# Layer-norm statistics of attention computed once ahead of the loop, and the queries' rms factor moved behind their up-projection

## The reference, cut to what matters

```python
x = x + attention(_layernorm(x))
x = x + ffn(_layernorm(x))
x = x + ssm(_layernorm(x))
x = x + ffn(_layernorm(x))

# attention, 16 heads, on the normed x
q_c    = _rms_norm(x @ wq_down.T, q_norm_w)          # 192 wide
q_nope = (q_c @ wq_up.T)                             # 128 per head
q_pe   = _apply_rope(q_c @ wq_rope.T, cos, sin)      # 64 per head
kv_c   = _rms_norm(x @ wkv_down.T, kv_norm_w)        # 64 wide
k_rope_shared = _apply_rope(x @ wk_rope.T, cos, sin) # 64 wide
out = softmax(causal(q k^T * scale)) v ; return out @ wo.T
```

## Time and profile before

| | us |
|---|---|
| median of 3 runs | 927.52 (922.5 to 929.87) |
| the profiled execution, its own time | 930.69 |
| its span, first to last instruction | 928.9 |
| mean granted clock of TensorE | 0.947 of full speed |

### The profile page before, as it was taken

How to read it: one execution, slowest core, us unless ns; L and a number is a source line. 1 busy time by engine, 2 the same in 40 slices (tenths; PEclk the granted TensorE clock), 3 DMA queues, 4 the chain that set the end, 5 groups by cost and what they waited for, 6 DMA issues and landing times.

```text
span 928.9 us, 17601 instructions
## 1 busy us (share of the span) xinstructions
PE 788.6 (85%) x4556; PEld 671.1 (72%) x4556; DVE 733.8 (79%) x2388; ACT 575.7 (62%) x1388; POOL 508.8 (55%) x545
## 2 busy tenths in 40 slices
PE   4768879889688898877989999988999956679998
PEld 4657658777577787765877788866888845568887
DVE  3768999899699899779989999976555678755555
ACT  3458767777566787665878789964333357433332
POOL 2599999999999999999999998100000000000000
PEclk9789999999889999888999999998999978789999
DMA  9600000000000000000000100000000000000000
GB/s 259 202 1 1 1 1 1 1 2 2 4 1 1 1 1 1 4 2 1 1 2 1 36 1 1 1 1 1 1 0 0 0 0 1 0 1 23 23 23 23
DMA packets 15393, 14.66 MB, mean 16 GB/s; under 512 B 5792, under 2 KB 14432, under 8 KB 15040
## 3 DMA queue, kind: packets, MB, share of 16 engines
q1 hardware_dynamic: 13792, 11.41, 4.2%
q0 software_dynamic: 624, 2.12, 0.7%
q10 hardware_dynamic: 880, 0.04, 0.1%
HBM read 11.46 MB, written 2.10 MB: 15 GB/s over the span
## 4 chain that ended last, share of the span: by engine, by line
PE 57%; DVE 21%; issue 14%; ACT 5%; DVEq 1%; DMA 1%; ACTq 0%; SPq 0%
PE bank L530 11%; PE bank L532 10%; PE bank L531 10%; PE bank L1280 5%; PE bank L1294 3%; DVE pt_lo L987 2%; PE bank L1297 2%; PE bank L1307 2%; PE bank L1309 2%; PE bank L1244 2%; DVE prob L978 2%; DVE bias_m L940 2%; DVE o_b L993 2%; PE bank L1255 1%; DVE q_tok L954 1%
## 5 line engine op out<-in xcount | busy, mean ns | idle before, releaser
L650 POOL TENSOR_SCALAR hot<-idx_gu,lut 128x256 f32<-128x256 bf16 x165 | 194.6, 1180 | 16.7
L700 ACT ACTIVATE prob<-bank,bias_m 128x128 f32<-128x128 f32 (+3 forms) x256 | 135.5, 529 | 49.7 <-DVE bias_m L940 48.4
L940 DVE CUSTOM_DVE_ANT_0 bank<-bank,mask 128x128 f32<-128x128 f32 (+3 forms) x256 | 126.0, 492 | 20.3 <-issue 18.5
L655 POOL TENSOR_TENSOR w_gu<-w_gu,hot 128x256 f32<-128x256 f32 x165 | 122.8, 744 | 13.8
L1280 PE MATMUL bank<-ident,prob 128*128 128x128 f32 x640 | 101.3, 282 | 22.0 <-issue 12.9
L727 ACT CAST pt_hi<-bank 128x512 fp32r<-128x512 f32 x160 | 93.7, 586 | 37.2 <-PE bank L1297 18.1
L987 DVE TENSOR_TENSOR pt_lo<-bank,pt_hi 128x512 fp32r<-128x512 f32 x160 | 108.9, 681 | 4.9 <-ACT pt_hi L727 4.6
L650 POOL TENSOR_SCALAR hot<-idx_dn,lut 128x256 f32<-128x256 bf16 (+1 forms) x90 | 98.1, 1090 | 9.1
L1280 PEld LDWEIGHTS bank<-ident,prob 128*128 128x128 f32 x640 | 75.9, 144 | 36.3 <-issue 22.0
L530 PE MATMUL bank<-kt_hi,qt_hi 128*128 128x128 f32 (+3 forms) x256 | 89.7, 351 | 10.0 <-ACT kt_hi L693 4.3
L807 ACT ACTIVATE silu<-bank 128x512 f32<-128x512 f32 x40 | 24.0, 599 | 99.0 <-PE bank L532 99.0
(11 more groups left out here) (196 smaller groups left out, 2249.1 us busy)
## 6 DMA issues: line engine op xcount, KB each, us to landing
x<-in_L_attn_a_x_dram SPq DMA_DIRECT2D x4, 512.0 KB, 7.9
wo_nat<-in_L_attn_a_wo_dram SPq DMA_DIRECT2D x1, 2048.0 KB, 12.3
out_dram<-x SPq DMA_DIRECT2D x16, 128.0 KB, 1.7
wqu<-in_L_attn_a_wq_up_dram SPq DMA_DIRECT2D x2, 768.0 KB, 7.5
wqr<-in_L_attn_a_wq_rope_dram SPq DMA_DIRECT2D x4, 192.0 KB, 7.6
raw_dn<-in_L_ffn_down_idx_dram POOLq DMA_DIRECT2D x1, 688.0 KB, 10.5
raw_gu<-in_L_ffn_gate_idx_dram POOLq DMA_DIRECT2D x1, 640.0 KB, 7.5
raw_gu<-in_L_ffn_up_idx_dram POOLq DMA_DIRECT2D x1, 640.0 KB, 8.2
```

The source lines that it names most:

```text
L650: nc.gpsimd.tensor_scalar(dst, idx[:, c:c + n], float(v), lut[:, v:v + 1], ALU.is_equal, ALU.mult).then_inc(lut_hot, 1)
L655: nc.gpsimd.tensor_tensor(w, w, hot[:, 0:n], ALU.add).then_inc(lut_sum, 1)
L700: nc.scalar.activation(prob[:, n % 2, h, 0:w], bank[2 + h % 2][:, 0:w], ACT.Exp, bias=bias_m[:, n % 2, h:h + 1], scale=-1.0, accum_out=den ...
L940: nc.vector.tensor_tensor_reduce(out=bank[2 + h % 2][:, 0:w], in0=bank[2 + h % 2][:, 0:w], in1=mask[:, TB * P - w:TB * P], scale=1.0, scal ...
```

## The change

1. New tiles hold statistics of all 16 token tiles. `at_stats_of(0, 1)` and `at_norm(0, 0, t)` take the place of `dve_ln(0, 0)`. After slot 1 of batch 0, `at_stats_of(1, BATCH)` runs bn_stats and bn_aggr on twelve tiles and the eleven-step square root once on twelve columns; then come batch 1's four normalisations. It waits there for the loads of batches 1 to 3, which were waited for ahead of slot 1's norm (batch 1) and ahead of the loop (2 and 3).
2. In the loop, slots 8 and 9 hold only the four normalisations (`at_norm`, in slot 9).
3. The norm of batch 0 for the feed-forward layer (number FIRST = 5) is computed in the last batch, four `ln_step`s behind each of slots 10 to 14, and its transposes, high and low parts behind slot 18. The loop's third pass still normalises and transposes batch 0 with its old statistics; nothing uses that.
4. `token_step` loses the four scalings of the query columns, and the four scalings of the key and value columns become two tensor_tensor over 128 x 256 with broadcast operands, the second of which waits for the first. 24 steps become 18.
5. `set_rq` copies the queries' four factors to r_q, after the preparation of batch 0 and in slot 15 of the loop. `q_copy` becomes an activation with r_q as its scale; the three products of `rope_q` become scalar_tensor_tensor with r_q as their scalar. Both wait for `set_rq` at unit 0.

```diff
+        def at_stats_of(b0, b1):
+            e, tiles = nc.vector, slice(b0 * TB, b1 * TB)
+            for t in range(b0 * TB, b1 * TB):
+                e.bn_stats(at_stats[:, t, :], x[:, t, :]).then_inc(at_bn, 1)
+            e.wait_ge(at_bn, b1 * TB)
+            settle(2 * G)
+            for t in range(b0 * TB, b1 * TB):
+                e.bn_aggr(at_mv[:, t, :], at_stats[:, t, :]).then_inc(at_agg, 1)
+            e.wait_ge(at_agg, b1 * TB)
+            c0 = 1 if b0 == 0 else RSQRT + 2
+            e.tensor_scalar(at_v[:, tiles], at_mv[:, tiles, 1], LN_EPS, None, ALU.add).then_inc(at_ref, 1)
+            for k in range(RSQRT):
+                rsqrt_step(k, at_ref, c0, at_v[:, tiles], at_r[:, tiles], at_t[:, tiles])
...
             def q_copy(b, n):
                 act.wait_ge(qa_mm, b * UNITS + n + 1)
                 free_after(act, qt_mm, b * UNITS + n - 1)
-                nc.scalar.copy(q_tok[:, n % 2, :, 0:KR], heads(bank[0])[:, :, 0:KR]).then_inc(qa_cp, 1)
+                if n == 0:
+                    act.wait_ge(rq_set, b + 1)
+                i = tile_of(n)
+                nc.scalar.activation(q_tok[:, n % 2, :, 0:KR], heads(bank[0])[:, :, 0:KR], ACT.Copy,
+                                     scale=r_q[:, i:i + 1]).then_inc(qa_cp, 1)
...
+                if s == 18:
+                    act_xt(FIRST)
...
-                elif n < TB:
-                    dve.wait_ge(rms_ref, c0 + RSQRT)
-                    nc.vector.tensor_scalar(cd[:, n, 0:QR], cd[:, n, 0:QR], rms_r[:, 2 * n:2 * n + 1], None, ALU.mult)\
-                        .then_inc(tok, 1)
-                elif n < 2 * TB:
-                    t = n - TB
-                    nc.vector.scalar_tensor_tensor(out=cd[:, t, QR:QR + KR], in0=cd[:, t, QR:QR + KR],
-                                                   scalar=rms_r[:, 2 * t + 1:2 * t + 2], in1=kvn[:, :],
-                                                   op0=ALU.mult, op1=ALU.mult).then_inc(tok, 1)
+                elif n < 2:
+                    kv = cd[:, :, QR:QR + KR]
+                    if n == 0:
+                        dve.wait_ge(rms_ref, c0 + RSQRT)
+                        by = rms_r[:, 1:2 * TB:2].unsqueeze(2).to_broadcast([P, TB, KR])
+                    else:
+                        dve.wait_ge(tok, 1 + TOK * b + 1)
+                        by = kvn[:, :].unsqueeze(1).to_broadcast([P, TB, KR])
+                    nc.vector.tensor_tensor(kv, kv, by, ALU.mult).then_inc(tok, 1)
...
-                nc.vector.tensor_tensor(q, raw, cs, ALU.mult).then_inc(q_rope, 1)
+                if n == 0:
+                    dve.wait_ge(rq_set, b + 1)
+                r = r_q[:, i:i + 1]
+                def turned(o, raw_, table):
+                    nc.vector.scalar_tensor_tensor(out=o, in0=raw_, scalar=r, in1=table, op0=ALU.mult, op1=ALU.mult)\
+                        .then_inc(q_rope, 1)
+                turned(q, raw, cs)
...
                     if s in (8, 9):
-                        if s == 8 and k == 0:
-                            dve.wait_ge(x_add[0], 1 + b * TB)
-                        ln_step(GAPS * (s - 8) + k, nb + 1, (nb + 1) % BATCH)
+                        if s == 9 and 3 <= k < 3 + TB:
+                            at_norm(nb + 1, (nb + 1) % BATCH, k - 3)
...
                 if s == 1:
-                    dve.wait_ge(x_in_s[1], 16)
-                    dve_ln(1, 1)
+                    for b in range(1, BATCH):
+                        dve.wait_ge(x_in_s[b], 16)
+                    at_stats_of(1, BATCH)
+                    for t in range(TB):
+                        at_norm(1, 1, t)
...
             for s in range(LEAD, UNITS + DEPTH):
                 dve_slot(s, BATCH - 1, None)
+                if s == 10:
+                    dve.wait_ge(x_add[0], 1 + TB)
+                if 10 <= s < 15:
+                    for k in range(4 * (s - 10), 4 * (s - 10) + 4):
+                        ln_step(k, FIRST, 0)
+                if s == 18:
+                    dve_xt(FIRST)
...
+                if s == 18:
+                    pe.wait_ge(qt_lo_s, 1 + BATCH * UNITS)
+                    pe.wait_ge(q_rope, 4 * BATCH * UNITS)
+                    pe_xt(FIRST)
+            wait_xt(pe, FIRST)
```

More of the change, by code:

```diff
@@ L120, in build @@
         rms_r = keep("rms_r", [P, TB * 2], F32)
+        at_stats = keep("at_stats", [P, BATCH * TB, 6], F32)
+        at_mv = keep("at_mv", [P, BATCH * TB, 2], F32)
+        at_v = keep("at_v", [P, BATCH * TB], F32)
+        at_t = keep("at_t", [P, BATCH * TB], F32)
+        at_r = keep("at_r", [P, BATCH * TB], F32)
+        r_q = keep("r_q", [P, TB], F32)
         bias_m = keep("bias_m", [P, 2, G], F32)
@@ L467, in build, with at_norm, rows @@
         LN_STEPS = TB + 1 + RSQRT + TB
+        FIRST = BATCH + 1
+        def at_stats_of(b0, b1):
[11 more added lines that the diff above has]
+                rsqrt_step(k, at_ref, c0, at_v[:, tiles], at_r[:, tiles], at_t[:, tiles])
+        def at_norm(p, xb, t):
+            e = nc.vector
+            e.wait_ge(xt_mm, 2 * p)
+            if t == 0:
+                e.wait_ge(at_ref, (RSQRT + 1) * (1 if isinstance(p, int) and p == 0 else 2))
+            def rows(m):
+                return m[:, bass.ds(xb * TB + t, 1)]
+            e.tensor_scalar(xn[:, t, :], rows(x).rearrange("p a d -> p (a d)"), rows(at_mv)[:, :, 0], rows(at_r),
+                            ALU.subtract, ALU.mult).then_inc(ln_norm, 1)
         def ln_step(k, p, xb):
@@ L473, in rows @@
                 return x[:, bass.ds(xb * TB + t, 1), :].rearrange("p a d -> p (a d)")
-            c0 = (RSQRT + 1) * p + 1
+            q = p - FIRST
+            c0 = (RSQRT + 1) * q + 1
             if k < TB:
@@ L492, in ln_step @@
                                 ALU.subtract, ALU.mult).then_inc(ln_norm, 1)
-        def dve_ln(p, xb):
-            for k in range(LN_STEPS):
-                ln_step(k, p, xb)
         def xt_bank(p, c):
-            return bank[(6 if isinstance(p, int) and p == 1 else 4) + c]
+            return bank[({1: 6, FIRST: 0}.get(p, 4) if isinstance(p, int) else 4) + c]
         def pe_xt(p):
@@ L882, in _ @@
             dve.wait_ge(x_in_s[0], 16)
-            dve_ln(0, 0)
+            at_stats_of(0, 1)
+            for t in range(TB):
+                at_norm(0, 0, t)
             dve_xt(0)
@@ L888, in _ @@
             half = ROPE // 2
-            TOKEN_STEPS = 1 + RSQRT + 2 * TB + 4
+            TOKEN_STEPS = 1 + RSQRT + 2 + 4
+            TOK = 8
             def token_step(k, b):
@@ L921, in token_step, with set_rq @@
                     nc.vector.tensor_tensor(kr, kr, k_rot[:, :, :], ALU.add).then_inc(tok, 1)
+            def set_rq(b):
+                dve.wait_ge(rms_ref, (RSQRT + 1) * (b + 1))
+                nc.vector.tensor_copy(r_q[:, :], rms_r[:, 0:2 * TB:2]).then_inc(rq_set, 1)
             def split_values(b):
@@ L953, in rope_q @@
                 free_after(dve, qt_mm, b * UNITS + n - 1)
-                nc.vector.tensor_tensor(q, raw, cs, ALU.mult).then_inc(q_rope, 1)
+                if n == 0:
[5 more added lines that the diff above has]
+                turned(q, raw, cs)
                 free_after(dve, q_rope, k)
-                nc.vector.tensor_tensor(q_rot[:, :, 0:half], raw[:, :, half:ROPE], s0, ALU.mult).then_inc(q_rope, 1)
-                nc.vector.tensor_tensor(q_rot[:, :, half:ROPE], raw[:, :, 0:half], s1, ALU.mult).then_inc(q_rope, 1)
+                turned(q_rot[:, :, 0:half], raw[:, :, half:ROPE], s0)
+                turned(q_rot[:, :, half:ROPE], raw[:, :, 0:half], s1)
                 dve.wait_ge(q_rope, k + 3)
@@ L1037, in dve_slot @@
                     do(rope_q, s)
+                    set_rq(nb)
                     feature_low(nb, 0)
@@ L1071, in _ @@
             split_values(0)
+            set_rq(0)
             dve.wait_ge(a_exp, 1)
@@ L1076, in _ @@
                 if s == 1:
-                    dve.wait_ge(x_in_s[1], 16)
-                    dve_ln(1, 1)
+                    for b in range(1, BATCH):
+                        dve.wait_ge(x_in_s[b], 16)
+                    at_stats_of(1, BATCH)
+                    for t in range(TB):
+                        at_norm(1, 1, t)
                 if s == 3:
                     dve_xt(1)
-            for b in range(2, BATCH):
-                dve.wait_ge(x_in_s[b], 16)
             with dve.Fori(0, BATCH - 1) as b:
```

55 lines of the change are left out of this document (29 added, 26 removed).

## The result

| | before | after |
|---|---|---|
| median of 10 runs, us | 927.94 (922.5 to 929.87) | 938.63 (933.73 to 939.73) |
| the profiled execution, its span | 930.69, 928.9 | 938.98, 937.2 |
| mean granted clock | 0.947 | 0.954 |

A forecast was written before the change was run, and what follows sets the result against it. DVE was taken to set loop slots 8 to 11 in the first pass, with PE also full in the last batch. Terms -9.3 - 6.9 + 8.0 + 2.5 + 6.4 + 2.0 + 0.6 = +3.3 us; forecast 930.5 us, range 917 to 941.

The forecast's parts named there:

- the rope's scalar: Rope products on DVE: 0.06 us per scalar, 11.7 us over 64 units, partly covered; +8.0 us, bounds 0 and 11.7.
- slots 8 and 9: Loop slots losing sixteen of twenty norm steps: 3.3 us saved in pass one, 3.0 in each other; -9.3 us.
- the clock lost in the last batch: Rival: DVE's uncovered norm idles PE in slots 10 to 14, the clock falls; 940 us, chance 0.13.
- no gain behind the jump: Rival: PE and the jump set slots 8 and 9 in passes two and three; 936.5 us, chance 0.12.
- The first rival: Slots 8 and 9 give all they can and shorter slots keep the clock up; 920 us, chance 0.20.
- Slots 10 and 11: Loop slots with shorter token steps on a full DVE: 2.3 us less a pass, -6.9 us for three passes.
- The fill: Batch 0: twelve tiles' statistics after slot 1 add 3.3 us, token steps save 0.8; +2.5 us, bounds 1 and 4.
- The last batch: Twenty norm steps come into slots 10 to 14, where DVE has no room; +6.4 us, bounds 5.8 and 7.8.
- the third rival: Last batch, slots 10 to 14: uncovered norm idles PE and the clock falls; 940 us, chance 0.13.
- Slot 18: Extra transposes, copies and subtractions behind slot 18 as the pipeline drains; +2.0 us, bounds 1.0 and 3.3.
- The free scalar: Rival: the rope's scalar costs nothing, as the number of instructions stays; 8.0 us less, 922.5 us, chance 0.05.
- `set_rq`: Copy of 128 x 4 on DVE in the loop's slot 15: 0.2 us, three times, +0.6 us.

The follow-up runs named there:

- POOL at rest: POOL's lookup cut from 16 values to 2: kernel before 899.47 us, with a column of ones as rope scalar 909.70 us, changed kernel 908.09 us.
- the statistics alone: Changed kernel with the token steps, query copy and rope products of the kernel before: 925.95 us, ratio 0.9972 to the kernel before.
- the queries' part: Kernel before with parts 4 and 5 of the change alone: 936.29 us, ratio 1.0085 to the kernel before.
- the scalar alone: Kernel before with the three rope products as scalar_tensor_tensor with a column of ones as scalar: 946.41 us, ratio 1.0184 to the kernel before.

## Why the prediction was right or wrong

The range held (938.6 us against 917 to 941), and the ratio of 1.0101 lies on the bound of 1% itself, with an interval that reaches to both sides of it. The predicted 930.5 was 8 us low. That it was not further off is luck: the rope's scalar cost 9 to 12 us more than its term, and slots 8 and 9 gave 7 us more than theirs. The prediction gave 0.19 to a time over 937 us, by the clock lost in the last batch or by no gain behind the jump, and neither happened. Of its signs, DVE's sum in attention was to be hardly changed, and grew by 6.8 us (516.0 to 522.8 up to the last rope addition); slot 9 of the first pass was to be 8 to 9 us with DVE not full, and took 10.3.

- **The rope's scalar (+8.0, bounds 0 to 11.7)** is the step that failed. The 0.06 us of L263 was right to a nanosecond or two. The cover was not: I let PE and ACT cover 1.1 us in slots 8 and 9, and took 2.6 us off for idle time of DVE in about half of the other slots. (As worded, a third less for half of them is 1.8 us, and the term 8.8.) With POOL at rest 39 of the loop's 49 slots grew by 0.14 to 0.21 us, the full price, and all 49 by 9.25; only the six slots 8 and 9 covered it (69.04 us before, 68.63 with the scalar). And the bound of 11.7 was none, for with POOL at work the loop grew by 5 us more. Measured alone: 17 to 18 us. The query copy on ACT was priced rightly at 0.1 us and at nothing in the time:

```profile
L707 ACT COPY q_tok<-bank 128x256 f32<-128x256 f32 x64 | 23.5, 368 | 3.2 <-PE bank L1248 3.2
...
L742 ACT ACTIVATE q_tok<-bank,r_q 128x256 f32<-128x256 f32 x64 | 30.1, 470 | 3.2 <-PE bank L1311 3.2
```

- **Slots 8 and 9 (-9.3, bounds 3.3 to 16.2).** The direction was right, the size was off: 16.3 us in the changed kernel, and 18.6 to 19.7 us without the rope, over the upper bound. The first pass gave 2.2 for 3.3 us. The error lay behind the jump, where I took 3.0 us from a clock of 0.85 as a sign that PE set the pace; it gave 7.8 and 9.6. DVE stands at the jump, then had 9.1 us of work to catch up, and PE waited and lost its clock for it. The low clock was a consequence of the work that left: with it gone, the clock there was 1.00 in both passes of the statistics alone. The first rival named this mechanism for slot 12, and put it at 4 us.
- **Slots 10 and 11 (-6.9).** 3.6 us in those slots by the queries' part against the scalar alone, -3.0 in the changed kernel with the rope in it. The two products cost the 0.4 us each that I took. What I removed was overpriced: L904 and L908 had 462 and 521 ns in the earlier trace rows, and with POOL at rest the same eight instructions take

```profile
L905 DVE TENSOR_SCALAR cd<-cd,rms_r 128x192 f32<-128x192 f32 x12 | 3.5, 309 | 0.0
L909 DVE SCALAR_TENSOR_TENSOR cd<-cd,rms_r,kvn 128x64 f32<-128x64 f32 x12 | 3.3, 273 | 0.0
```

  So 1.6 of the 3.9 us that I counted in a pass was waiting for POOL, and this came back elsewhere: in the same token steps of the changed kernel

```profile
L471 DVE SCALAR_TENSOR_TENSOR rms_r<-rms_t,rms_r 128x8 f32<-128x8 f32 x9 | 3.2, 360 | 0.0
L957 DVE TENSOR_TENSOR k_rot<-cd,sin 128x128 f32<-128x128 f32 x6 | 2.2, 402 | 0.0
```

  take 360 and 402 ns for 218 and 280 before. With POOL at rest the three passes gave 0.7 us in all. Slot 11 ended at 9.94 us, not 9.
- **The fill (+2.5, bounds 1 and 4).** The change measured +5.9. The block behind slot 1 was costed well:

```profile
55.76 4.01 DVE L482 BATCH_NORM_STATS2 at_stats<-x 128x6 f32<-128x256 f32 x12
...
64.41 1.94 DVE L501 TENSOR_SCALAR xn<-x,at_mv,at_r 128x256 f32<-128x256 f32 x4
66.27 2.47 DVE L345 TENSOR_TENSOR wo_b<-bank,wo_a 64x512 fp32r<-64x512 f32 x4
```

  10.51 us to L345 for the 6.77 us of before, +3.7 for my 3.3, and PE's wait for it went from 3.4 us to 7.1:

```profile
PE bank L335 <- DVE wo_b L345: 7.1, 1, 7.1
```

  The token steps of batch 0 gave 0.9 for 0.8. What I left out is the clock, for PE was granted half its speed for 10.2 us from 65 us on, where the kernel before had two stretches of 3.4 us, and the rope's price in the fill, which the scalar alone puts at 3 to 4 us by the end of slot 7.
- **The last batch (+6.4, bounds 5.8 and 7.8).** Slots 11 to 15 grew by 6.0 us, slots 9 to 15 by 7.4, of which the scalar alone has 1.2. Right. The clock stayed at 1.00 there, so the third rival, whose 940 us lie nearest to the measurement, was not what happened; of its sum only the 3.7 us of a rope without cover came true.
- **Slot 18 (+2.0).** The last two residual additions of attention lie 22.81 us apart for 20.25: +2.6, within the bounds.
- **The free scalar**, by the rule of the Trainium skill in "VectorE: DVE Perf Modes", section "Rules for kernel authors", is refuted here: the count of instructions stayed and each cost 0.06 us more on the engine and 0.09 in the time.
- **No gain behind the jump** is refuted by its slots. `set_rq` took 159 ns in the loop, three times, for the 0.6 us of its term.

## What to carry to other kernels

A full PE beside a full DVE covers nothing: where two engines hand work to each other once a slot and both are full, added time of either is on the path, so multiply an added operand by all such slots and discount nothing. A duration read beside a busy POOL holds waiting that removing the instruction needn't remove; where DVE works beside a POOL loop of long instructions, price DVE edits by an experiment. The same loop in half the chunk gave this attention back 17 us, and cost the whole kernel 120, since POOL then ended last. A removed block was worth most here where the pipeline had to catch up, and the low clock there was what the block did, not what limited its removal.

## What was not expected of the hardware

- A per-partition scalar from SBUF costs a DVE instruction on PSUM and SBUF operands 59 to 61 ns, for 128 and 256 columns alike; by 64 units, three a unit came to 17 to 18 us with POOL at work and 10.2 us at rest in the whole time, and to 19.6 and 13.6 us by the end of the last rope addition.
- POOL at work cost this attention 30.9 us of 594, and 13.5 of 577 when its instructions were about half as long.
- POOL's tensor_tensor held a DVE addition of two SBUF inputs until 0.28 us behind its own end; POOL's tensor_scalar of 1.15 us let the 28 that started 0.31 us or more behind its start pass in 0.42 or 0.43 us.
- 22 one-column memsets in the gaps of two DVE-heavy slots cost nothing that could be measured.
